# Raw tokens kept in SBUF, and state steps and inter-chunk sets ahead of each quad's first scores

## What is computed

```python
xn = layernorm(x)
# linear attention: 16 heads of 8, chunks of 64 tokens
q, k, v = split(xn @ W_qkv); k = layernorm_noaffine(k)
def step(S, chunk):
    inter = einsum('bhde,bthe->bthd', S, q_c)
    scores = where(causal, einsum('bthd,bshd->bhts', q_c, k_c), 0)
    intra = einsum('bhts,bshd->bthd', scores, v_c)
    return S + einsum('bthd,bthe->bhde', v_c, k_c), inter + intra
attn = y @ W_o
# experts: each token goes to the one of 8 whose centroid it is nearest to
h = relu((ln(xn) * ln_g[e] + ln_b[e]) @ w1[e].T + b1[e])      # 128 -> 512
ffn = xn + sigmoid(xn @ centroids[e]) * (h @ w2[e].T + b2[e])
out = x + attn + ffn
```

## Time and profile before

| what | us |
|---|---|
| median of 3 runs | 363.84 (362.66 to 364.79) |
| span of the profiled execution | 362.3 |
| busy: TensorE matmul, weight load | 341.5 (94%), 293.6 (81%) |
| busy: VectorE, ScalarE, GpSimd | 283.4 (78%), 242.3 (67%), 250.6 (69%) |
| DMA moved | 33.18 MB, mean 92 GB/s |

### The profile page before, as it was taken

How to read it: one execution, slowest core, us unless ns; L and a number is a source line. 1 busy time by engine, 2 the same in 40 slices (tenths; PEclk the granted TensorE clock), 3 DMA queues, 4 the chain that set the end, 5 groups by cost and what they waited for, 6 DMA issues and landing times.

```text
span 362.3 us, 17501 instructions
## 1 busy us (share of the span) xinstructions
PE 341.5 (94%) x6868; PEld 293.6 (81%) x6868; DVE 283.4 (78%) x799; ACT 242.3 (67%) x657; POOL 250.6 (69%) x245
## 2 busy tenths in 40 slices
PE   7798999989999999999999989999999999999991
PEld 6466787767687687778868878999999999999990
DVE  8887898897785887977878786788877778777760
ACT  4787687777577667666665735766777767766660
POOL 3488477898797865455555503888888888888884
PEclk9999999999999999999999999999999999999997
DMA  7220333536314031445453435555555555555420
GB/s 196 70 62 19 105 91 112 178 104 187 105 48 120 26 99 52 149 131 159 132 158 94 133 86 144 67 74 71 69 69 71 72 73 69 71 76 60 36 24 0
DMA packets 55153, 33.18 MB, mean 92 GB/s; under 512 B 5352, under 2 KB 52768, under 8 KB 55072
## 3 DMA queue, kind: packets, MB, share of 16 engines
q1 hardware_dynamic: 42800, 23.53, 23.5%
q0 software_dynamic: 12272, 8.54, 17.1%
HBM read 18.72 MB, written 13.78 MB: 90 GB/s over the span
## 4 chain that ended last, share of the span: by engine, by line
issue 26%; PE 18%; POOL 12%; DVE 1%; ACT 1%; POOLq 1%; DVEq 0%; ACTq 0%
POOL out_dram L494 12%; PE sc L1274 4%; PE bank L1328 3%; PE bank L1337 2%; PE bank L1222 2%; PE bank L1200 1%; PE bank L1306 1%; PE bank L1295 1%; PE bank L1209 1%; PE bank L1215 1%; POOLq L71 1%; PE bank L1255 1%; DVE pr L856 1%; PE bank L1228 1%; PE bank L1233 1%
## 5 line engine op out<-in xcount | busy, mean ns | idle before, releaser
L494 POOL DMA_INDIRECT out_dram<-qx,rows x71 | 112.7, 1588 | 36.2 <-issue 21.9
L694 ACT ACTIVATE qx<-sc,b1T 128x128 f32<-128x128 f32 x280 | 80.0, 368 | 39.6 <-PE sc L1421 39.4
L420 POOL DMA_INDIRECT slots_d<-rows,pos_i x64 | 63.1, 986 | 40.6 <-PE bank L1328 10.3
L856 DVE TENSOR_TENSOR pr<-sc,causal 128x1536 f32<-128x1536 f32 (+2 forms) x33 | 63.5, 1926 | 16.1 <-PE sc L1274 16.0
L1429 PE MATMUL bank<-tokens,qx 128*128 128x128 f32 x568 | 75.2, 275 | 0.7 <-ACT qx L694 0.7
L1421 PE MATMUL sc<-wide,tokens 128*128 128x128 f32 x560 | 74.0, 275 | 0.5 <-issue 0.5
L1429 PEld LDWEIGHTS bank<-tokens,qx 128*128 128x128 f32 x568 | 69.0, 192 | 1.1 <-ACT qx L694 1.1
L1421 PEld LDWEIGHTS sc<-wide,tokens 128*128 128x128 f32 x560 | 68.2, 192 | 0.6 <-issue 0.6
L1015 DVE COPY tokens<-xT 128x1024 f32 x71 | 52.8, 745 | 0.0
L1030 DVE SCALAR_TENSOR_TENSOR qx<-bank,rows,qx 128x128 f32<-128x128 f32 x71 | 24.8, 349 | 27.2 <-PE bank L1429 26.2
L1274 PEld LDWEIGHTS sc<-qx,kT 32*64 32x64 f32 x2048 | 32.9, 130 | 15.5 <-issue 15.0
(11 more groups left out here) (167 smaller groups left out, 530.7 us busy)
## 6 DMA issues: line engine op xcount, KB each, us to landing
rows<-slots_d SPq DMA_DIRECT2D x71, 66.0 KB, 2.1
res<-in_L_attn_x_dram SPq DMA_DIRECT2D x16, 256.0 KB
out_dram<-res SPq DMA_DIRECT2D x16, 256.0 KB, 3.6
tokens<-in_L_attn_x_dram SPq DMA_DIRECT2D x7, 512.0 KB, 4.2
w1raw<-in_L_ffn_w_dram SPq DMA_DIRECT2D x8, 256.0 KB
w2raw<-in_L_ffn_w_dram SPq DMA_DIRECT2D x8, 256.0 KB
out_dram<-qx,rows POOLq DMA_INDIRECT x71, 3.4
slots_d<-rows,pos_i POOLq DMA_INDIRECT x64
```

The lines of the kernel that those rows point to most:

```text
L420: pool.indirect_dma_start(slots_d, bass.IndirectOffsetOnAxis(ap=pos_i[:, t:t + 1], axis=0), rows[:, t, :], None)\
L494: pool.indirect_dma_start(out_rows, bass.IndirectOffsetOnAxis(ap=xs[:, a, D + 2:D + 3].bitcast(U32), axis=0), ye[:, a, :], None, bounds_ch ...
L694: last = nc.scalar.activation(ht[:, k % 2, c * P:(c + 1) * P], inner(k)[:, c * P:(c + 1) * P], ACT.Relu, bias=b1T[:, bass.ds(e * FC + c, 1)])
L856: nc.vector.tensor_tensor(pr[:, h % 2, a:G, w].rearrange("p g (j t) -> p g j t", t=CH), sc[:, a * BANK:G * BANK].rearrange("p (g w) -> p g ...
```

## The change

The raw tokens get a tile for all eight columns and stay there; `load_resid` and its buffer go, the add for the residual works in place in the token tile and the stores go from there. The two broadcast tables and, at the end, the weights of the expert stage lie in columns that have been stored. SP's loads and stores are paced by q's and v's products.

`FA` and `FB` become one tile of two banks, into which the state step writes both parts, and one `dstate_copy` evicts both. The x and weight transposes go to the score banks 2 and 3, behind the mask of the quad's second scores. TensorE's order becomes: scores(2n), q of the next quad (behind the output in quads 3, 5, 7, 9, which rank tokens), products(2n - 1), k transposes, output(n - 1), scores(2n + 1), products(2n), affinities, v, kT of the quad after the next, transposes, state_step(n + 1), inter_second(n), inter_first(n + 1). VectorE evicts the state before the mask and always adds the residual in the first half; ScalarE copies q first and expands from that copy.

The diff, cut to its core:

```diff
-        tokens = sb("tokens", [P, 3 * WE])
-        xin = tokens[:, 0:2 * B * D].rearrange("p (a b d) -> p a b d", a=2, b=B)
-        ws = tokens[:, :].rearrange("p (a w) -> p a w", a=3)
+        CW = B * D
+        tokens = sb("tokens", [P, NCH * CW])
+        xin = tokens[:, :].rearrange("p (c b d) -> p c b d", c=NCH, b=B)
+        b2b = tokens[:, 0:E * D].rearrange("p (e d) -> p e d", d=D)
+        lbb = tokens[:, CW:CW + E * D].rearrange("p (e d) -> p e d", d=D)
+        ws = tokens[:, 2 * CW:2 * CW + 3 * WE].rearrange("p (a w) -> p a w", a=3)
+        WSC = 2 + (3 * WE + CW - 1) // CW
...
-        banks = [ctx.enter_context(nc.psum_tensor(f"bank{i}", [P, BANK], F32)) for i in range(4)]
-        FA, FB, Y = banks[0], banks[1], banks[2:4]
+        fab = ctx.enter_context(nc.psum_tensor("fab", [P, 2 * BANK], F32))
+        FA, FB = fab[:, 0:BANK], fab[:, BANK:2 * BANK]
+        banks = [FA, FB]
+        Y = [ctx.enter_context(nc.psum_tensor(f"y_bank{i}", [P, BANK], F32)) for i in range(2)]
+        XA, XB = SC[2], SC[3]
...
+        def ranked(n):
+            return n in (3, 5, 7, 9)
...
-                sp.dma_start(xin[:, c % 2, :, :], x_v[:, c, :, :]).then_inc(s(f"x_in{c + 1}"), 16)
-            def load_resid(n):
-                half = n % 2
-                reach(sp, s(f"attn_out{half}"), 16 * (n // 2))
-                sp.dma_start(res[:, half, :, :], x_v[:, n // 2, half * HALF:(half + 1) * HALF, :])\
-                  .then_inc(s(f"resid_in{half}"), 16)
...
-                sp.dma_start(out_v[:, c, half * HALF:(half + 1) * HALF, :], res[:, half, :, :])\
+                sp.dma_start(out_v[:, c, half * HALF:(half + 1) * HALF, :], xin[:, c, half * HALF:(half + 1) * HALF, :])\
...
+                e = n - 5 if 5 <= n < 5 + RAW else n - 9 + RAW if n >= 9 and n - 9 + RAW < E else None
+                sp.wait_ge(s("q_ps"), n + 2)
+                if n + 4 < NCH:
+                    load_tokens(n + 4)
+                if n == 6:
+                    stored(n - 1)
+                    sp.dma_start(lbb, ln_b.partition_broadcast(P)).then_inc(s("lb_in"), 16)
+                if n == 8:
...
+                if e is not None:
+                    load_w1(e)
                 if n:
                     store_quad(n - 1)
...
-                mask_scores(h)
-                if h % 2 == 0:
+                if h % 2 == 0 and h:
                     state_middle(n)
                     state_end(n)
+                mask_scores(h)
+                if h == 0:
+                    state_middle(0)
+                    state_end(0)
...
+            for n in range(LATE, NQ):
+                pool.wait_ge(s("sc_ps"), 2 * n + 1)
                 send_rows(1)
...
+                pool.wait_ge(s("av_ps"), 2 * n)
+                send_rows(2)
+                pool.wait_ge(s("av_ps"), 2 * n + 1)
+                send_rows(4)
...
-                if h % 2 and more:
-                    q_expand(n + 1, 0)
-                    q_expand(n + 1, 1)
-                if h and by_act(h):
-                    score_copy(h)
                 if h % 2 == 0:
-                    if more:
-                        kT_copy(n + 1)
+                    if h and by_act(h):
+                        score_copy(h)
                     if norm:
                         ln_root(n + 2)
+                    if more and not ranked(n):
+                        q_copy(n + 1)
                     if n:
                         y_copy(n - 1)
                     if more:
                         kn_copy(n + 1)
+                        if ranked(n):
+                            q_copy(n + 1)
                         k_square(n + 1)
-                    if norm:
-                        ln_norm(n + 2, (5, 6))
+                        q_expand(n + 1, 0)
                     if n in (2, 4, 6, 8):
                         second_root(n // 2 - 1)
                 else:
                     if more:
                         k_root(n + 1)
-                        for j in range(2, J):
-                            q_expand(n + 1, j)
+                        q_expand(n + 1, 1)
+                    if by_act(h):
+                        score_copy(h)
+                    if norm:
+                        ln_norm(n + 2, (5, 6))
+                    if more:
+                        q_expand(n + 1, 2)
+                        q_expand(n + 1, 3)
                     if n < 8 and n % 2 == 1:
                         affT_copy(n // 2)
-                    if more:
-                        q_copy(n + 1)
-                    if more:
-                        values_across(n + 1)
+                    if n and n + 2 < NQ:
+                        kT_copy(n + 2)
                     if norm:
-                        xT_copy(2 * n + 2, FA)
-                        xT_copy(2 * n + 3, FB)
+                        xT_copy(2 * n + 2, XA)
+                        xT_copy(2 * n + 3, XB)
                     elif n - 7 < E:
                         w1_copy(n - 7)
                         w2_copy(n - 7)
+                    if n == 0:
+                        kT_copy(2)
+                    if more:
+                        values_across(n + 1)
                     if more and n + 1 >= LATE:
                         values_own(n + 1)
...
+            def dstate_copy(n):
                 dve.wait_ge(s("ds_ps"), n + 1)
                 reach(dve, s("smid_ready"), n)
-                nc.vector.tensor_tensor(dstate[:, 0, :, :], Y[n % 2][:, 0:HALF * GW].rearrange("p (i k) -> p i k", k=GW),
-                                        bcast(smask[:, :], 1, HALF), ALU.mult).then_inc(s("dsta_sb"), 1)
-            def dstate_second(n):
-                reach(dve, s("state_ready"), n)
...
-                dve.wait_ge(s(f"resid_in{half}"), 16 * (n // 2 + 1))
-                nc.vector.tensor_tensor(res[:, half, :, :], Y[n % 2][:, :].rearrange("p (i d) -> p i d", d=D),
-                                        res[:, half, :, :], ALU.add).then_inc(s("res_ready"), 1)
+                x_rows = xin[:, n // 2, half * HALF:(half + 1) * HALF, :]
+                nc.vector.tensor_tensor(x_rows, Y[half][:, :].rearrange("p (i d) -> p i d", d=D), x_rows, ALU.add)\
+                    .then_inc(s("res_ready"), 1)
...
+                    if n:
+                        dstate_copy(n)
+                    score_mask(h)
+                    if n == 0:
+                        dstate_copy(n)
...
-                    if n and out_early(n):
+                    if n:
                         result(n - 1)
...
-                    if n and not out_early(n):
-                        result(n - 1)
...
+            def turned(n):
+                if n + 1 < NCH:
+                    pe.wait_ge(s("xT_sb"), 2 * n + 4)
+                elif n - 7 < E:
+                    pe.wait_ge(s("w1_sb"), n - 6)
+                    pe.wait_ge(s("w2_sb"), n - 6)
...
-                    second_left(n - 2)
+                    pe.wait_ge(s("qT_sb"), n)
                 pe.wait_ge(s("xT_sb"), n + 1)
-                mm(FB[:, :], wqkv[:, D:2 * D], xT[:, HALF * n:HALF * (n + 1), :].rearrange("p i t -> p (i t)"), start=True,
+                mm(FB if n < 2 else FA, wqkv[:, D:2 * D], xT[:, HALF * n:HALF * (n + 1), :].rearrange("p i t -> p (i t)"), start=True,
                    stop=True).then_inc(s("kT_ps"), 1)
...
+                if n:
+                    pe.wait_ge(s("dst_sb"), n)
...
-                bank_y_free(n)
-                if n == 0:
-                    pe.wait_ge(s("qT_sb"), 1)
-                    pe.wait_ge(s("xT_sb"), 2)
-                else:
-                    first_left(n - 1)
-                if n == 1:
-                    pe.wait_ge(s("small_sb"), 2)
-                if n in (3, 5, 7, 9):
-                    rank_tokens(n // 2 - 1)
+                pe.wait_ge(s("qT_sb"), n + 1)
+                pe.wait_ge(s("kT_sb"), min(n + 2, NQ))
                 for i in range(HALF):
                     for a in range(P // GW):
...
+                    if n:
+                        turned(n - 1)
...
-            for h in range(NH):
-                n = h // 2
+            for n in range(NQ):
                 more = n + 1 < NQ
                 norm = n + 1 < NCH
-                scores(h)
-                if h % 2 == 0:
-                    if more:
-                        kT_project(n + 1)
-                    state_step(n)
-                    if h:
-                        products(h - 1)
-                    inter_first(n)
-                    if more:
-                        k_transpose(n + 1)
-                    if n and out_early(n):
-                        output(n - 1)
-                    if more:
-                        q_project(n + 1)
+                scores(2 * n)
+                if n == 0:
+                    kT_project(1)
+                    state_step(0)
+                elif more and not ranked(n):
+                    q_project(n + 1)
+                if n:
+                    products(2 * n - 1)
```

(53 more changed lines are left out.)

127 lines of the change are left out of this document (48 added, 79 removed).

## The result

The changed kernel takes 386.3 us (median of 4 runs, 385.9 to 389.1), against 363.3 us for the kernel before on the same chip: a ratio of 1.064, with a 95% interval of 1.060 to 1.068. The forecast was 369.3 with a range up to 373.0. So the sign was right and the size was not: 23.0 us of loss (22.5 against the 363.84 that the forecast started from) instead of 5.5.

What follows compares the result with a forecast made beforehand. TensorE was taken to bound the kernel before, VectorE's loop many quads after; quad lengths summed to 208.3 us, 3.5 over 204.77, plus 1.0 for late scores and 1.0 for stalls: 5.5, giving 369.3 us, range 361.3 to 373.

Steps and rivals of the forecast that it cites:

- The loop: VectorE's mask to v scaling, then state step, inter-chunk sets and scores: 9.8 plus 3.1 us, taken as 12.95, in late quads.
- its long scores: Late scores are 1.43 us long against 1.21 early; in the loop of five quads this adds 1.0 us.
- Rival 1: TensorE keeps the pace, VectorE's stretch from mask to v scaling staying under 9.0 us: 361.6 us; chance 0.21.
- "Issue" stalls at 1.0 (0 to 3.9): TensorE's 3.9 us of stalls inside product groups before the change add 1.0 us, as slack covers most in the loop's quads.
- Rival 3: "Issue" stalls stay whole inside the loop, 2.9 us more, or last scatters hold up slot loads: 373 us; chance 0.12.
- The slack "some 0.8 us": In the loop's quads TensorE's slack ahead of its state step covers most of a stall there.
- The start, 17.15: Quad 0's chain has no slack; kT copy, state step, eviction, transposes and q put quad 1's scores at 30.1 us.
- ScalarE's work "0": ScalarE's work stays the same and its q expansions behind the copy cost 0, next scores being most of a quad away.
- Odd quads, 13.35 each: Quads 1, 3, 5, 7: TensorE sets them, 13.20 us by clean quad 7 plus 0.15 for the moved output.
- The last two quads, 11.5 and 10.9: Quad 14, without routing and with half a state, 8.3 plus 3.1; quad 15, first scores to first expert product, 10.9 us.
- The expert stage at 0: From 225 us on TensorE is always busy and its instructions and order are unchanged, so the stage keeps its length.
- Residual loads at 0: 16 loads of 256 KB go; their wait was never last, so this is worth 0.

Runs made afterwards that it cites:

- 6: Changed kernel with VectorE's result add and bias fold moved behind the v scaling: 382.2 us, ratio 1.052.
- 9: Changed kernel with both inter-chunk sets ahead of the state step, chunk 1's directly behind the v product: 379.2 us, ratio 1.042.
- 2: Changed kernel with runs of short products appended, alone or with one or two 512-column products per 64 pairs: 128 dense pairs took 3.7 to 4.0 us.
- 3: Changed kernel with ten transposes filling TensorE's first gap, ahead of the first state step: 385.8 us, quad 0 17.36 us.
- 7: Changed kernel with ScalarE's last two expansions of q moved behind the copies of kT and of the transposes: 385.5 us, ratio 1.059.
- 12: Changed kernel with one extra 512-column product ahead of the first scores of quads 1 to 15: 393.8 us, ratio 1.083.
- 5: Kernel before, in its own order and banks, with only the raw tokens kept on chip: 363.8 us against 363.9, ratio 0.9995.
- 1: Changed kernel with state step and inter-chunk sets back behind the first scores, state eviction behind the mask, q behind the output: 394.4 us, ratio 1.080.
- 11: Changed kernel with the moves of 6 and 7, quad 1's kT copy ahead of the value copies, and chunk 1's set behind v: 388.8 us, ratio 1.069.
- 14: Changed kernel with the first scores of quads 1 to 15 computed twice in a row: 416.3 us, ratio 1.143.

## Why the prediction was wrong, point by point

- **The loop: right.** In quad 13, with 0.7 us of stalls, VectorE's rows above show it: 10.2 + 2.9 = 13.0 us against 9.8 + 3.1 = 12.95. Quads 10, 11 and 12 took 12.7, 14.6 and 13.8, with 1.3, 1.8 and 1.5 of stalls in them, and quad 9 14.7 against 14.0, with 2.3. Taking the add and the fold out of the loop gave 4.1 us (6), taking the sets out of its tail a part of 7.1 (9). I had put the loop and its long scores at 4.7 us. Rival 1's sum, 361.6, doesn't use its own 12.1 throughout; with it quad 9 gives 1.9 and quads 10 to 13 give 3.4, which is 360.9. Nothing hangs on that, as the loop was there.
- **"Issue" stalls at 1.0 (0 to 3.9): the term that failed.** In the view that gave the 3.9 they are 13.0 us now; at block ends they are 19.2 where they were 6.4, 12.8 more. I carried them over as a sum of the kernel before, where they were five, and even its upper bound was only their not being covered. But they are a function of the order. Before, the kT product stood between scores and state step, and q between k's transposes and scores. After, state step, two sets and scores are 32, 16, 16 and 64 pairs: 128 in a row, one block, in 2.7 us of work, where 3.7 is the pace (2). The longest such row before was scores and products, also 128, and the order after has both. In the rows of before the mark was there: all stalls in mid-group, with no releaser. Rival 3 had their place (in the loop) but the same bound. The lengths of the 16 quads less these stalls are 205.7 us; the forecast without its stall term had 209.3. So, as it seems, some 3.6 us of the stalls went into slack or into lengths that I had put too long, and the rest is what the sum lacked.
- **The slack "some 0.8 us" ahead of the state step: too small to cover them.** The 13 longer ones are 0.5 to 1.7 us each, and some fall in the scores, behind the slack, in the loop's tail (quad 11).
- **The start, 17.15: 19.0.** The order of steps was right; 1.6 of the 1.85 missed is TensorE's clock after two gaps (3: 17.36). I had timed its steps at the full clock.
- **ScalarE's work "0": wrong, but small.** State steps wait for the copy of kT 6.0 us, 2.4 and 0.8 of it in quad 0. In quads 2, 4, 6 and 8 it is 0.41, 0.91, 1.03 and 0.48: the variance comes late from VectorE, its root stands ahead of expansions and copy, and the copy now is last. Its order alone gave 0.8 (7).
- **Odd quads, 13.35 each: 14.1 to 15.3.** The stalls of the second point lie in them, 0.6, 2.0, 1.1 and 1.3 us, 1.46 of it at 61.18, in quad 3; less these they are 13.1 to 13.9, so the length without stalls was nearly right. Taking the sets apart gave 1.8 in quad 3 (9). They were 13.2 to 14.9 before too, and I had put them below that, from the one clean quad of them; with their own lengths the sum would have been 2.3 us higher.
- **The last two quads, 11.5 and 10.9: 12.6 and 12.6.** A stall of 1.1 us lies in quad 14, at 220.60, and 1.6 and 1.4 us in quad 15, at 227.34 and 235.25. With 0.7 and 1.4 us of stalls instead of 3.0 the last quad is 10.6 (9) and 11.1 (12), so the 10.9 was not too short for its own work.
- **The expert stage at 0: +1.9.** It ends by GpSimd's scatters. Their group in the kernel before, and in the changed one:

```profile
L494 POOL DMA_INDIRECT out_dram<-qx,rows x71 | 112.7, 1588 | 36.2 <-issue 21.9 <-DVE qx L1030 14.2
```
```profile
L490 POOL DMA_INDIRECT out_dram<-qx,rows x71 | 114.4, 1611 | 36.4 <-issue 21.3
```

  71 times 0.023 is 1.6 us. The kernels 5 (1587 ns) and 1 (1590 ns) have the old length, 144.3; all others here have the new, 1610 to 1616. VectorE's copies in this stage (71 of 1024 elements) go with them in part: 745 ns on average before, 748 in 5, 767 in 1, 780 to 792 in the others. 1 has the changed banks and tiles, so these alone are not the cause. What is stays open.
- **Residual loads at 0: right** (5).

What stays open besides: why the packet of a block starts 4.2 to 4.8 us late in four blocks of the changed kernel. All four have v's product (three of them kT's too) and transposes near their beginning and the dense row behind them. That this order delays the packet wasn't tried by itself.

## What to carry to other kernels

Before you reorder a kernel of many short matmuls, look at its "issue" gaps inside groups: if they lie a fixed number of instructions apart, the program's supply is a resource with a pace, and an order that puts short groups side by side costs time though no data is late. Here dense rows of 128 pairs came every 3.7 to 4 us, and with a long product in each every 3.5 to 3.75; spread long products between the short groups. And a set that stands ahead of a wait is its cover: count what it covers on each engine before you move it, since moves that are harmless each by itself may together take it away (7 and 9 against 11).

## What was unexpected of the hardware

- TensorE's program came in blocks of 256 instructions, one 16 KB packet each; in the profiles of all sixteen kernels no block was entered within 2.17 us of its packet's start and no two packets started within 3.23 us, and 128 dense pairs took 3.7 to 4.0 us instead of 2.1, at either level of the clock. With this go 7.5 us of time for 15.9 us of added work (12), and 30.0 for 17.1 (14).
- Products of 64 x 64 that all write one place took 60 ns a pair; those of a state step, to four places in turn, 0.69 us for 32 pairs. Whether the one place is the cause wasn't tried.
- 4.2 MB less of DMA traffic changed neither the time (ratio 0.9995) nor the stalls at block ends (6.1 against 6.4).
